# Transposes of the next batch's normed rows moved from behind the values of quad 0 to directly behind the query, key and value units

## The reference

```
x = layernorm(x + L0_attn(x))          # four recurrent layers over the tokens, post-normed
x = layernorm(x + xattn(x, ctx, mask)) # 16 heads of 64: q = x Wq, k, v = ctx Wkv
x = layernorm(x + ffn(x))              # 8-bit rows, ternary weights, 1024 hidden

sim  = clip(where(mask, q k^T / 8, -max), -5, 5)
out  = softmax(sim) v
xattn = out Wo + bo
ffn  = bitlinear(silu(bitlinear(x, w_gate)) * bitlinear(x, w_up), w_down)
```

## Time and profile before

| | us |
|---|---|
| median of 3 runs | 3654.46 |
| lowest, highest | 3654.07, 3657.61 |
| the profiled execution | 3654.35 |
| its span | 3652.6 |
| PE busy | 3518.5 |
| DVE busy | 3414.1 |
| ACT busy | 3045.7 |
| POOL busy | 2311.6 |

### The profile page before, as it was taken

How to read it: one execution, slowest core, us unless ns; L and a number is a source line. 1 busy time by engine, 2 the same in 40 slices (tenths; PEclk the granted TensorE clock), 3 DMA queues, 4 the chain that set the end, 5 groups by cost and what they waited for, 6 DMA issues and landing times. The chain is left out here.

```text
span 3652.6 us, 168847 instructions
## 1 busy us (share of the span) xinstructions
PE 3518.5 (96%) x71457; PEld 2338.8 (64%) x71489; DVE 3414.1 (93%) x9400; ACT 3045.7 (83%) x6636; POOL 2311.6 (63%) x2515
## 2 busy tenths in 40 slices
PE   5999999999999999999999977999999999999997
PEld 3666666666666666666666654666666666666665
DVE  8999999999999999999999987999999999999997
ACT  4999999999999999999999965767776767777775
POOL 3777777777777777777777737555555555555552
PEclk9999999999999999999999998999999999999998
DMA  2000222000011010111001100000000000000000
GB/s 83 26 25 26 57 60 56 26 26 26 25 26 27 26 26 26 26 27 26 25 26 25 27 28 18 25 25 25 25 25 25 27 30 28 25 25 25 24 8 10
DMA packets 99980, 104.35 MB, mean 29 GB/s; under 512 B 17296, under 2 KB 95004, under 8 KB 98728
## 3 DMA queue, kind: packets, MB, share of 16 engines
q1 hardware_dynamic: 99224, 93.56, 9.0%
HBM read 48.52 MB, written 17.53 MB: 18 GB/s over the span
## 5 line engine op out<-in xcount | busy, mean ns | idle before, releaser
L572 POOL TENSOR_TENSOR conv_products<-normed_features,conv_taps_by_token 128x256 f32<-128x256 f32 (+1 forms) x837 | 758.2, 921 | 597.7 <-ACT normed_features L355 419.6
L299 PE MATMUL banks<-up_centred,after_cell_features 128*32 128x336 f32 x8928 | 684.2, 446 | 4.0 <-DVE after_cell L534 3.7
L783 POOL TENSOR_TENSOR exps_of_both_halves<-scores 128x256 f32<-128x256 f32 x512 | 404.5, 815 | 427.3 <-ACT scores L1062 424.8
L299 PEld LDWEIGHTS banks<-up_centred,after_cell_features 128*32 128x32 f32 x8928 | 302.2, 109 | 299.8 <-issue 245.6
L306 PE MATMUL banks<-down,hidden_features 112*32 112x256 f32 x6696 | 420.8, 383 | 0.2
L1062 ACT ACTIVATE scores<-scores 128x512 f32<-128x512 f32 x512 | 302.8, 624 | 81.4 <-DVE scores L1213 81.4
L394 ACT ACT_TABLE_LOAD x279 | 358.0, 1283 | 4.9
L373 ACT ACT_TABLE_LOAD x279 | 358.0, 1283 | 4.9
L585 POOL TENSOR_TENSOR conv_partial_sums<-conv_products,conv_partial_sums 128x512 f32<-128x512 f32 x279 | 358.4, 1284 | 0.0
L1213 DVE SCALAR_TENSOR_TENSOR scores<-banks,score_top 128x512 f32<-128x512 f32 x512 | 317.3, 681 | 6.4 <-PE banks L888 3.0
L273 PE MATMUL banks<-recurrent_weights,h_features 64*32 64x256 f32 x8928 | 313.8, 380 | 0.0
(11 more groups left out here) (224 smaller groups left out, 9946.5 us busy)
## 6 DMA issues: line engine op xcount, KB each, us to landing
layer_inputs<-layer_outputs SPq DMA_DIRECT2D x279, 96.0 KB, 2.1
layer_inputs<-in_x SPq DMA_DIRECT2D x280, 32.0 KB, 1.8
x_scratch<-layer_outputs SPq DMA_DIRECT2D x279, 32.0 KB, 2.1
x_tokens<-in_x SPq DMA_DIRECT2D x32, 256.0 KB, 3.1
context_features<-in_ctx SPq DMA_DIRECT2D x32, 256.0 KB, 3.7
layers_out<-x_scratch SPq DMA_DIRECT2D x32, 256.0 KB, 2.8
out<-result SPq DMA_DIRECT2D x64, 128.0 KB, 1.8
up_centred<-in_ff_up SPq DMA_DIRECT2D x1, 2688.0 KB
```

What stands on the lines that cost most here:

```text
L299: mm = nc.tensor.matmul(bank[group(l), b, 0:UP], xmt[:, n, group(l)], up[:, l, n, at:at + UP], start=n == 0, stop=n == HALF - 1, skip_grou ...
L572: return nc.gpsimd.tensor_tensor(prod[:, i:i + n], xnt[:, j % NRING].rearrange("p n t -> p (n t)")[:, None, :].broadcast_to([P, n, HALF * ...
L783: nc.gpsimd.tensor_tensor(psum[:, i % RING, :], pr[:, i % RING, 0:S], pr[:, i % RING, S:2 * S], ALU.add).then_inc(halves_added, 1)
```

## The change

On TensorE the call `x1_features(j + 1)` moves from behind `attend(j, 0, 1)` to in front of the loop over the quads, so directly behind the last unit (in batch 0 behind the first batch's own opening steps, the last of which is the small matmul of L1006). It passes `scores(j, 1)`, both halves of the values of quad 0 and its denominators. No instruction is added or removed, no wait is changed, and the order on VectorE, ScalarE, GpSimd and SyncE is the same as before.

```diff
                     scores(j, 0)
                     unit(j, SPLIT + 2)
                     unit(j, SPLIT + 3)
+                if j + 1 < B:
+                    x1_features(j + 1)
                 for q in range(QUADS):
                     if q + 1 < QUADS:
                         scores(j, q + 1)
                     attend(j, q, 0)
                     denominators(j, q)
                     attend(j, q, 1)
-                    if q == 0 and j + 1 < B:
-                        x1_features(j + 1)
                     if q == 3 and j > 0:
                         transpose_h(f, 1)
```

## The result

The changed kernel takes 3661.61 us in the median, against 3654.95 us for the kernel before in the same comparison: 1.0017 times as long, with a 95% interval of 1.001 to 1.0024, or 6.2 us more (3.7 to 8.8). One of its 18 executions ran at a mean granted clock of 0.557 in place of 0.99 and took 5902.76 us; the ratio leaves it out. The forecast of 3664.7 was 3 us too high.

The account below looks back on a forecast made before the run. The prediction took TensorE to set the pace (196.12 of 200 us busy), with VectorE nearly as full. A 0.34 us lateness in each of 30 batches summed to 10.2 us, giving about 3664.7; the range was 3651 to 3669.

Parts of the forecast that it names:

- TensorE alone, -0.10: Transposes on TensorE: 0.49 us more at the new place, 0.59 given back at the old, so -0.10 a batch.
- the lower bound of 0.39: Least extra time a batch for the transposes at the new place on TensorE: 0.39 us; the upper bound was 0.59.
- `attended` +0.49: VectorE's attended of quad 0 starts 0.49 us later, 47.67 to 48.16, its 0.56 wait unable to take this up.
- The add ahead of `h_round_up`: Quad 0: GpSimd's add starts 0.11 us ahead of h_round_up and holds it, so clip 8 starts 0.34 later.
- 0.34 goes through: From clip 8 through later clips to hidden_features and feed_out's second half: the whole 0.34 us lengthens the batch.
- rival 2: VectorE's clips 8 to 15 partly take up the lateness, leaving 0.05 to 0.2 a batch, about 3658 us; chance 0.14.
- The weight load waits 0.3 longer: TensorE's weight load before feed_out's second half waits 0.3 us or more longer than 0.26.
- Batch 0 at nothing: Batch 0 costs nothing, as TensorE stands 6.63 us for GpSimd's adds; without that cover, 2 us once.
- The sum: Whole second stage: 30 batches at 0.34 us each, 10.2 us more, giving about 3664.7 us.
- the forecast's own band: Loss of 0.25 to 0.45 us a batch, +7.5 to +13.5 us in all, 3662 to 3668; chance 0.50.
- The rule of the Trainium skill: VectorE and GpSimd block each other at h_round_up; without blocking, only TensorE's -3.0 us would remain, so it spoke against the change.

Follow-up runs that it names:

- Behind the denominators: Against the changed kernel, the transposes stand between the denominators of quad 0 and the second half of its values; 3671.17 us, 1.0048 of the kernel before.
- `h_round_up` first at the old place: Kernel before, with only h_round_up of the first half moved ahead of attended of quad 0; 3654.56 us, 0.9997 of the kernel before.
- `both first` at the new place: Changed kernel with h_round_up of both halves moved ahead of attended, in quads 0 and 2; 3646.16 us (0.9976), run again 3649.33 us (0.9980).
- `both first, old place`: Kernel before, transposes unmoved, with h_round_up of both halves moved ahead of attended in quads 0 and 2; 3651.16 us, 0.9988 of the kernel before.

## Why the prediction was right, and where it was not

- **TensorE alone, -0.10.** Right in sign, and a little too small. The transposes cost 0.43 at the new place, not 0.49: behind them the scores start after 0.53, not 0.59, near the lower bound of 0.39. So TensorE is 0.16 ahead at the scores of quad 2 and not 0.10. What is left of it in a batch once `h_round_up` is first is 0.08 to 0.10.
- **`attended` +0.49.** Measured +0.43, by the same term. The wait stayed 0.56, as said: it can't take up lateness whose cause also makes its releaser late.
- **The add ahead of `h_round_up`.** As said for quad 0: the add at 48.61 (said: 48.66), `h_round_up` at 48.71 (48.77), 1.18 long (1.19), clip 8 +0.27 (+0.34). That it ends 0.56 behind the end of the add it meets held in quad 0 of every kernel (0.54 to 0.56). But that the batch pays *because* the add is late was too narrow. Behind the denominators the adds were on time and the loss was three times as large, because a late `attended` met the next add. Since `h_round_up` was held before as well, the meeting made the lateness smaller at the new place, from 0.43 to 0.27. No run takes the meeting away altogether.
- **0.34 goes through.** Mis-sized. Of 0.27, 0.19 reached `hidden_features` and 0.18 the batch. The 0.08 went at clip 12, in the room that rival 2 named (the scores' arrival at clip 12). Before, clip 12 started at 54.06, just when the scores of quad 3 set it free: with `h_round_up` first at the old place it waited 0.80 us for them and started at 54.05. After, it starts 0.21 late.
- **The weight load waits 0.3 longer.** Wrong: it stayed 0.26. The prediction had itself written that the denominators of quad 1 go late (0.3; measured 0.16) and TensorE's gain is gone; it didn't carry this on. TensorE comes to `feed_out` 0.19 late, and ScalarE as late. A wait between two engines shows only their difference, and both were late from one cause.
- **Batch 0 at nothing.** It was 1.7 us shorter in this execution, for a reason that was not in the sum (below).
- **The sum.** 0.18 x 30 = 5.4 in place of 10.2. Between the forecast's own band (0.25 to 0.45) and rival 2 (0.05 to 0.2 a batch) the measured 0.18 is rival 2's; the time of 3661.61 lies just under the foot of the band in us. The stated range holds it because it took rival 2 in. The forecast had the sign and the way from the new place to `attended` and clip 8 right; the sizes of what reaches clip 8 and of what goes through from there were too large, and the wait at its end was wrong.
- **The rule of the Trainium skill** (Advanced Engine Details and Errata, Mode Summary: the second Vector port is shared with GpSimd, and GpSimd's instructions and Vector's in a two-port mode block each other) told rightly that `h_round_up`, over 0.56 behind the add's end, would not be over 0.56 behind its own start here: it took 1.18. It was no reason for the loss by itself: there was a loss with an add late and with the adds on time.

Why 0.08 to 0.10 and not 0.16 of TensorE's gain remains can be read from the rows, though no run tried it apart. The weight load of the denominators of quad 1, `both first` at the new place, then at the old:

```profile
2848.00 0.16 PEld L910 LDWEIGHTS banks<-exps_of_both_halves,ones_for_sums 128*32 128x32 f32 x8 [0.34 <-POOL exps_of_both_halves L783]
```

```profile
2846.86 0.25 PEld L910 LDWEIGHTS banks<-exps_of_both_halves,ones_for_sums 128*32 128x32 f32 x8 [0.18 <-POOL exps_of_both_halves L783]
```

On the scale of before (2848.00 and 2.25, 2846.86 and 3.39) both weight loads start at 50.25, because GpSimd's last add ends at 50.20 in both. TensorE is 0.16 ahead at the scores of quad 2, 0.10 at those of quad 3, and still 0.10 at `feed_out` (62.78 and 62.88): the rest of the lead is spent waiting for the adds.

## What to carry over

Before moving a step on the fullest engine, look for the nearest *waiting* instruction of the next fullest one behind both places. If its releaser stands between them, a good part of the move's length can be paid there (0.18 of 0.43 here, 0.56 of 0.59 at the worst place), however little the step costs its own engine. First put independent work into that wait; then the place can be chosen by its own cost. Such work need not gain anything where the step stands now: at the old place it gave nothing. And a wait that stays the same length doesn't prove that nothing is later: compare both sides from a common point.

## What the hardware showed

**The engine that is well ahead goes first, and the other's waiting is recorded as work.** In batch 0 VectorE's L1422 and GpSimd's L805, both on 128x2048 elements, meet more than once; this is the meeting where the kernels differ. VectorE and GpSimd before, then `both first, old place`, whose batch 0 has the same instructions in the same order:

```profile
2217.04 2.34 DVE L1422 SCALAR_TENSOR_TENSOR ff_ternary<-ff_raw,ff_half_mean,ff_ternary 128x2048 bf16<-128x2048 f32 x1
```

```profile
2217.20 7.48 POOL L805 TENSOR_SCALAR ff_ternary<-ff_raw,ff_minus_half_mean 128x2048 bf16<-128x2048 f32 x1
```

```profile
2218.91 4.73 DVE L1422 SCALAR_TENSOR_TENSOR ff_ternary<-ff_raw,ff_half_mean,ff_ternary 128x2048 bf16<-128x2048 f32 x1
```

```profile
2217.78 5.44 POOL L805 TENSOR_SCALAR ff_ternary<-ff_raw,ff_minus_half_mean 128x2048 bf16<-128x2048 f32 x1
```

With VectorE 0.16 us ahead it takes 2.34 and GpSimd 7.48; with VectorE 1.13 behind, GpSimd takes 5.44 and VectorE 4.73. GpSimd is longer by 2.04, about the 2.18 us in which both run: it was held for about that time. VectorE is longer by 2.39, though both run for 4.31: it was held for a part of it only. In the steady batches a lead of 0.04 was not enough for VectorE (1.34 long). Where between 0.04 and 0.16 it turns, and whether it depends on the instruction, was not tried.

**What decided it, by the rows, was TensorE's clock.** Ahead of this meeting TensorE makes the denominators and the second half of the values of quad 1, for which VectorE's L1298 and so L1422 wait. These values before, after, and in `both first, old place`:

```profile
2215.24 1.05 PE L898 MATMUL banks<-scores,v_tokens 128*32 128x256 f32 x16
```

```profile
2219.64 1.93 PE L898 MATMUL banks<-scores,v_tokens 128*32 128x256 f32 x16
```

```profile
2216.23 1.93 PE L898 MATMUL banks<-scores,v_tokens 128*32 128x256 f32 x16
```

And the stretches they stand in, before and after (the last three columns are the granted clock as a share of 2.4 GHz, the DMA share and GB/s):

```profile
2214.70:2216.30 1.60, 1.51 (x25) 0.76 (x26) 0.00 (x0) 0.78 (x3) 1.60 (x3) 1.00 0.00 0
```

```profile
2218.70:2221.50 2.80, 2.72 (x24) 0.99 (x24) 0.00 (x0) 1.54 (x4) 2.80 (x5) 0.50 0.00 0
```

The granted clock is 1.00 (2.4 GHz) before and 0.50 (1.2 GHz) after: the 16 matmuls take 1.93 in place of 1.05. TensorE had stood 3.25 us for GpSimd before and 3.61 after just ahead of it. The slower matmuls (0.88 us in the values, 0.44 in the denominators ahead of them) make VectorE 1.3 us later: from 0.16 ahead of L805 it comes to 1.12 behind. It is then held by GpSimd, and GpSimd, which TensorE waits for next, is over with L805 2 us earlier (5.43 in place of 7.48): by these rows, a slower clock made the batch 1.7 us *shorter*. In all twelve profiled executions the pair agrees: batch 0 of 60.04 to 60.07 us goes with 1.93, 61.75 to 61.80 with 1.05. No run sets the clock by itself, so this is read from rows, not tried. The place of the transposes of batch 0 goes with it but doesn't fix it: all six profiled executions with them at the new place show 1.93, and of the four with them at the old place three show 1.05, but `both first, old place` has the slow clock, with a stand of only 2.71 us.
